# Expert feed-forward on one core: the 64 rest rows of the down product as 64-row products of two row tiles side by side

## The chip, the cores and the metric

The kernel runs on one core of one Trainium2 chip. The metric is the device time of the whole program in microseconds; the median of three runs before the change is 769.99 us (768.62 to 772.36).

## The reference

Cross attention, then a mixture of experts with a residual around each. Only the second half is touched.

```python
x = x + _L0_xattn_ref(_layernorm(x), ctx_2048, mask)          # 16 x 112 tokens of 512
# mixture of experts on the 1792 normed tokens: E = 64, TOP_K = 8, F_INT = 192
probs = softmax(x @ gate_weight.T); top_val, top_idx = lax.top_k(probs, 8)
...                                                           # some experts are rerouted to a similar one
gu = lax.ragged_dot(xs, swapaxes(gate_up_proj, 1, 2), group_sizes)    # 512 -> 2 x 192
gate, up = split(gu, 2)
hact = silu(gate) * up                                        # 192 inner columns for each row
y = lax.ragged_dot(hact, swapaxes(down_proj, 1, 2), group_sizes)      # 192 -> 512
out = zeros.at[tok].add(y * w[:, None])
```

## The kernel before

A first phase (to about 180 us) does the attention, the gate and the choice of experts for 16 batches, and writes a list of tokens and weights for each expert into a table in HBM. A short plan ranks the experts by their number of tokens. The second phase then goes through 63 experts in order of rank; each is a **unit**. `SIZES` gives a unit its number of row tiles `nt` and the rows `m` of a tile: 2 units of 3 x 128, 8 of 3 x 112, 7 of 3 x 96 (17 units of three tiles), then 17 of 2 x 128, 16 of 2 x 112, 12 of 2 x 96 and 1 of 2 x 80 (46 units of two tiles). One more unit of one tile of 128 rows for overflow runs in a loop at the end.

For a unit, SyncE loads the expert's weights into rings of buffers (`load_w1`: three parts of 256 KB into `raw1`, four buffers deep; `load_w2`: 256 KB and 128 KB into `raw2`, three deep). GpSimd gathers the token rows by the list (`gather`) and adds the results back to HBM with an accumulating scatter (`scatter`). Products are made in fp32r with every operand split into a high and a low part, so that each product is a sum of three: high by high, high by low, low by high. ScalarE makes the high parts (`w1_high`, `w2_high`, `h_high`, `x_high`), VectorE the low ones by subtraction (`w1_low`, `w2_low`, `h_low`, `x_low`).

TensorE runs through its program in order: transposes of the token rows (`turn_rows`), 36 products for gate and up (`gate_up`, L1256 to L1258), and, one unit later, the down products (`down`). The order in a round r is: turn rows of unit r+1, `gate_up` of r, `down` of r-1. Each engine has its own program of the same kind, written out by hand, and semaphores connect them. SyncE's program in round r is: list of r+6, w1 of r+4, w2 of r+3; the last waits until VectorE is through `w2_low(r)` (L931).

The inner size is 192 = 128 + 64 (`FR = 64`). The first 128 inner rows of a down tile are three products of 128 rows (L1269 to L1271). The 64 **rest rows** are packed to 128: `hh[:, 1]` holds the high part of h twice (partitions 0 to 63 and 64 to 127, since `h_rest` writes h twice), and `w2h[:, 1]` the high part of the rest weights in partitions 0 to 63 and their low part in 64 to 127. One product of 128 rows (L1273) is thus high by high plus high by low; a second one (L1274) has the low part of h for both. A tile of the down product is five products of 128 rows by 512 columns into one PSUM bank (`y_bank`, a ring of three); ScalarE empties the bank with `y_out` (L1061).

Of the kernel before, what the change touches and what calls it, by code (L numbers as in the profile page):

```python
# [24 lines left out]
F32 = mybir.dt.float32  # L25
F32R = mybir.dt.float32r
# [5 lines left out]
P = 128  # L32
B, T, D = 16, 112, 512
# [7 lines left out]
FR = F - P  # L41
# [28 lines left out]
RAW1, RAW2, LISTS, XGS = 4, 3, 12, 4  # L70
# [76 lines left out]
def program(nc, x, ctx, ctxT, mask, gwT, w1, w2a, w2b, sim, out):  # L147
# [4 lines left out]
    with ExitStack() as stack:  # L152
        def sb(name, shape, dt=F32):
            return stack.enter_context(nc.sbuf_tensor(name, shape, dt))

        def two(name, shape, dt=F32):
            return [sb(f"{name}{i}", shape, dt) for i in range(2)]
# [67 lines left out]
        raw2 = [sb(f"raw2_{i}", [P, 2, D]) for i in range(RAW2)]  # L225
        w1h = [sb("w1h0", [P, DK, 2 * F], F32R)]
        w1l = [sb("w1l0", [P, DK, 2 * F], F32R)]
        w2h = [sb("w2h0", [P, 2, D], F32R)]
        w2l = [sb("w2l0", [P, D], F32R)]
# [33 lines left out]
        early.close()  # L263
        w2h.append(sb("w2h1", [P, 2, D], F32R))
        w2l.append(sb("w2l1", [P, D], F32R))
        w1h.append(sb("w1h1", [P, DK, 2 * F], F32R))
        w1l.append(sb("w1l1", [P, DK, 2 * F], F32R))
        xh = two("xh", [P, DK, WIDE], F32R)
# [3 lines left out]
        hh = two("hh", [P, 2, WIDE], F32R)  # L272
        hl = two("hl", [P, 2, WIDE], F32R)
# [28 lines left out]
        def split_wait(eng, s, value):  # L302

            wait(eng, s, value)
            if not isinstance(value, int):
                eng.sem_inc(spacer, 1)

        def wait(eng, s, value):

            if not isinstance(value, int) or value > 0:  # L310
                eng.wait_ge(s, value)
# [56 lines left out]
        LAST = Unit(STATIC)  # L368
# [5 lines left out]
        def y_bank(u, t):  # L374
            return bank[5 + (u.tile + t) % 3]

        def freed_before(u, t, ring):

            return u.t0 + t if u.loop else max(u.t0 + t - ring + 1, 0)
# [13 lines left out]
        def over_loop(eng, late, early):  # L393

            overs = overs_of(eng)
            with eng.Fori(0, overs) as g:
                late(Unit(STATIC, g))
                early(Unit(STATIC, g + 1))
            return overs
# [5 lines left out]
        def _(sp):  # L405
# [55 lines left out]
            def weights_of(u):  # L461
                at = bass.ds(u.n - STATIC + 2 * E + MAX_OVER, 1) if u.loop else (
                    slice(E + u.n, E + u.n + 1) if u.n < STATIC else slice(2 * E + MAX_OVER, 2 * E + MAX_OVER + 1))
                return sp.value_load(prow[0:1, at], min_val=0, max_val=E - 1)
# [26 lines left out]
            def load_w2(u):  # L491
                split_wait(sp, w2l_s, u.units_freed(RAW2))
                e = weights_of(u)
                sp.dma_start(raw2[u.on(RAW2)][:, 0, :], w2a[bass.ds(e, 1)].rearrange("a p f -> (a p) f")).then_inc(w2_in[u.on(RAW2)], 16)
                sp.dma_start(raw2[u.on(RAW2)][0:FR, 1, :], w2b[bass.ds(e, 1)].rearrange("a p f -> (a p) f")).then_inc(w2_in[u.on(RAW2)], 16)

            load_w1(Unit(0))
            load_w1(Unit(1))
            load_w2(Unit(0))
            load_w1(Unit(2))  # L500
            load_w2(Unit(1))
            load_w1(Unit(3))
            load_w2(Unit(2))
            first_lists = [list_of(Unit(n)) for n in range(3)]
            for i in range(4):
# [18 lines left out]
            overs = over_loop(sp, lambda u: None, next_over)  # L524
# [3 lines left out]
            sp.wait_ge(merged, 16)  # L528
            split_wait(sp, list_in[LAST.on(LISTS)], (overs + LAST.turn(LISTS) + 1) * 16)
            split_wait(sp, w1_in[LAST.on(RAW1)], (overs + LAST.turn(RAW1) + 1) * 16 * W1_PARTS)  # L530
            split_wait(sp, w2_in[LAST.on(RAW2)], (overs + LAST.turn(RAW2) + 1) * 32)
            split_wait(sp, gathered[LAST.on(XGS)][0], (overs + LAST.turn_of_tile(XGS, 0) + 1) * 16)


# [131 lines left out]
        def _(dve):  # L666
            v = nc.vector
# [257 lines left out]
            def w2_low(u):  # L925
                dve.wait_ge(w2h_s, u.n + 1)
                wait(dve, y_ps, u.tiles_freed(2))
                b = u.on(2)
                raw = raw2[u.on(RAW2)]
                v.tensor_tensor(w2l[b][:], raw[:, 0, :], w2h[b][:, 0, :].bitcast(F32), ALU.subtract)  # L930
                v.tensor_tensor(w2h[b][FR:P, 1, :], raw[0:FR, 1, :], w2h[b][0:FR, 1, :].bitcast(F32),  # L931
                                ALU.subtract).then_inc(w2l_s, 1)

            w1_low(Unit(0))
# [2 lines left out]
            for r in range(STATIC):  # L937
                if r < RAMP:
                    stage(h_gate, r)
                    early_stage(x_low, r + 1, (0, 1))  # L940
                    stage(h_rest, r)
                    early_stage(x_low, r + 1, (2,))
                else:
                    early_stage(x_low, r + 1, (0, 1))
                    stage(h_gate, r)
                    early_stage(x_low, r + 1, (2,))
                    stage(h_rest, r)
                stage(w2_low, r)
                early_stage(w1_low, r + 2)
                stage(h_low, r)  # L950

            def late(u):
                h_gate(u)
                h_rest(u)
                w2_low(u)
                h_low(u)
# [9 lines left out]
        def _(act):  # L966
            a = nc.scalar
# [105 lines left out]
                a.copy(w1h[u.on(2)][:].rearrange("p c f -> p (c f)"), raw1[u.on(RAW1)][:]).then_inc(w1h_s, 1)  # L1073

            def w2_high(u):
                act.wait_ge(w2_in[u.on(RAW2)], (u.turn(RAW2) + 1) * 32)
                wait(act, y_ps, u.tiles_freed(2))
                b = u.on(2)
                raw = raw2[u.on(RAW2)]
                a.copy(w2h[b][:, 0, :], raw[:, 0, :])  # L1080
                a.copy(w2h[b][0:FR, 1, :], raw[0:FR, 1, :]).then_inc(w2h_s, 1)

            w1_high(Unit(0))
            w1_high(Unit(1))
# [1 line left out]
            for r in range(STATIC):  # L1086
                if r < RAMP:
                    stage(silu_gate, r)
                    early_stage(x_high, r + 1, (0, 1))
                    stage(w2_high, r)  # L1090
                    stage(silu_rest, r)
                    early_stage(x_high, r + 1, (2,))
                else:
                    early_stage(x_high, r + 1, (0, 1))
                    stage(silu_gate, r)
                    early_stage(x_high, r + 1, (2,))
                    stage(w2_high, r)
                    stage(silu_rest, r)
                early_stage(w1_high, r + 2)
                stage(h_high, r)  # L1100
                stage(y_out, r - 1)
            y_out(Unit(STATIC - 1))

            def late(u):
                silu_gate(u)
                w2_high(u)
                silu_rest(u)
                h_high(u)
                y_out(u)
# [9 lines left out]
        def _(pe):  # L1119
# [141 lines left out]
            def down(u):  # L1261
                b = u.on(2)
                pe.wait_ge(hl_s, u.n + 1)
                pe.wait_ge(w2l_s, u.n + 1)
                for t in range(u.nt):
                    wait(pe, ys_s, freed_before(u, t, 3))
                    s = slice(t * u.m, (t + 1) * u.m)
                    o = y_bank(u, t)[0:u.m, :]
                    pe.matmul(o, hh[b][:, 0, s], w2h[b][:, 0, :], start=True, stop=False)  # L1269
                    pe.matmul(o, hh[b][:, 0, s], w2l[b][:], start=False, stop=False)  # L1270
                    pe.matmul(o, hl[b][:, 0, s], w2h[b][:, 0, :], start=False, stop=False)  # L1271

                    pe.matmul(o, hh[b][:, 1, s], w2h[b][:, 1, :], start=False, stop=False)  # L1273
                    pe.matmul(o, hl[b][:, 1, s], w2h[b][:, 1, :], start=False, stop=True).then_inc(y_ps, 1)  # L1274

            turn_rows(Unit(0), (0, 1, 2))
            for r in range(STATIC):
                if r < RAMP:
                    stage(gate_up, r, 0)
                    stage(gate_up, r, 1)  # L1280
                    early_stage(turn_rows, r + 1, (0, 1))
                    stage(gate_up, r, 2)
                    early_stage(turn_rows, r + 1, (2,))
                else:
                    early_stage(turn_rows, r + 1, (0, 1))
                    stage(gate_up, r, 0)
                    early_stage(turn_rows, r + 1, (2,))
                    stage(gate_up, r, 1)
                    stage(gate_up, r, 2)
                stage(down, r - 1)  # L1290
            down(Unit(STATIC - 1))

            def late(u):
                for m in range(3):
                    gate_up(u, m)
                down(u)
# [42 lines left out]
```

## Time and profile before

| | |
|---|---|
| median of three runs | 769.99 us |
| the profiled execution: its time, its span | 767.57 us, 765.8 us |
| PE, matmul | 661.4 us busy (86%) |
| DVE, ACT, POOL | 542.6 us (71%), 456.7 us (60%), 541.9 us (71%) |
| granted TensorE clock over the span | 0.936 |
| DMA moved | 189.97 MB, mean 248 GB/s |
| raw<-in_w2b (the rest weights) | 65 loads of 128 KB |
| five down products L1269 to L1274 | about 144 of each |

The span is the time from the first to the last instruction of the profiled execution. PE is TensorE's matmuls, PEld its weight loads, SPq the queue of SyncE, which issues the weight loads. A matmul's own length contains the passage through the array, so neighbours overlap; what a product costs in a stream is the distance from its start to the next one's start.

### The profile page before, as it was taken

Reading aid. Unit: us, or ns where it says so; the run is one execution under the profiler, and the core shown is the slowest. Engines: PE = TensorE matmul, PEld = TensorE weight load, DVE = VectorE, ACT = ScalarE, POOL = GpSimd, SP = SyncE. Lnnn points to the kernel's source line nnn. Section 1 sums busy time; section 2 is a strip of 40 time slices with the busy share of each in tenths; the row PEclk is TensorE's granted clock in tenths of the full one; section 3 lists DMA queues with packets and bytes.
Section 4 is the critical chain, followed back from the end, with each engine's and each line's share of the span. In section 5 each row is a group of like instructions: output and inputs, shape, how many; then the busy total and the mean of one; then the engine's idle time right before and its main releaser. Section 6 shows DMA issues by size and latency. Waiting matters only on the chain. (4 is left out here: it accounts for less than half of the span.)

```text
span 765.8 us, 15219 instructions
## 1 busy us (share of the span) xinstructions
PE 661.4 (86%) x4278; PEld 554.9 (72%) x4278; DVE 542.6 (71%) x1213; ACT 456.7 (60%) x891; POOL 541.9 (71%) x463
## 2 busy tenths in 40 slices
PE   4999999831079999999999999999999999999920
PEld 2565555531069988888889999999999999889720
DVE  5598998865047666666677888888887887788611
ACT  3454454312036667667677877778777877768611
POOL 7007777777675877787788888878877888888521
PEclk9999999955579999999999999999999999999975
DMA  8999998615377999999999999999999999999576
GB/s 300 359 326 319 326 349 287 238 44 173 88 208 174 250 230 228 238 227 243 233 246 269 302 289 296 282 273 278 275 274 270 276 274 270 266 273 272 101 143 152
DMA packets 107589, 189.97 MB, mean 248 GB/s; under 512 B 33537, under 2 KB 35457, under 8 KB 106097
## 3 DMA queue, kind: packets, MB, share of 16 engines
q1 hardware_dynamic: 74274, 125.61, 52.0%
q0 software_dynamic: 33232, 63.39, 38.4%
q8 instruction: 35, 0.57, 0.3%
q14 instruction: 48, 0.39, 0.1%
HBM read 143.43 MB, written 56.24 MB: 261 GB/s over the span
## 5 line engine op out<-in xcount | busy, mean ns | idle before, releaser
L1256 PE MATMUL bank<-xh,w1h 128*128 128x256 f32 (+7 forms) x768 | 225.9, 294 | 3.6 <-issue 2.1
L1258 PE MATMUL bank<-xh,w1l 128*128 128x256 f32 (+7 forms) x768 | 220.0, 286 | 0.0
L1257 PE MATMUL bank<-xl,w1h 128*128 128x256 f32 (+7 forms) x768 | 219.9, 286 | 0.0
L617 POOL DMA_INDIRECT xg<-normed_tokens,list x145 | 170.9, 1179 | 59.6 <-issue 55.4
L601 POOL DMA_INDIRECT list_table<-token,slot x112 | 111.6, 996 | 74.4 <-issue 73.7
L626 POOL DMA_INDIRECT out_rows<-ys,list x73 | 123.1, 1686 | 39.7 <-issue 20.1
L1256 PEld LDWEIGHTS bank<-xh,w1h 128*128 128x128 f32 x768 | 147.0, 191 | 4.3 <-issue 4.2
L1257 PEld LDWEIGHTS bank<-xl,w1h 128*128 128x128 f32 x768 | 147.3, 192 | 0.1
L1258 PEld LDWEIGHTS bank<-xh,w1l 128*128 128x128 f32 x768 | 146.9, 191 | 0.0
L626 POOL DMA_INDIRECT second_sum<-ys,list x70 | 117.6, 1680 | 30.3 <-issue 18.6
L922 DVE TENSOR_TENSOR w1l<-raw,w1h 128x1536 fp32r<-128x1536 f32 x65 | 114.3, 1759 | 17.7 <-ACT w1h L1073 16.2
L916 DVE TENSOR_TENSOR xl<-bank,xh 128x448 fp32r<-128x448 f32 (+3 forms) x145 | 84.2, 617 | 50.4 <-ACT xh L1068 48.4
L1235 PE MATMUL bank<-ident,xg 112*128 112x112 f32 (+3 forms) x580 | 71.2, 264 | 52.1 <-DMA xg<-normed_tokens,list 48.5
L1073 ACT CAST w1h<-raw 128x1536 fp32r<-128x1536 f32 x65 | 95.6, 1471 | 30.5 <-DMA raw<-in_w 30.3
L1235 PEld LDWEIGHTS bank<-ident,xg 112*128 112x128 f32 (+3 forms) x580 | 62.7, 143 | 65.7 <-issue 33.7
L1068 ACT CAST xh<-bank 128x448 fp32r<-128x448 f32 (+3 forms) x145 | 69.9, 530 | 57.9 <-PE bank L1235 57.9
L1061 ACT ACTIVATE ys<-bank,list 112x512 f32<-112x512 f32 (+3 forms) x143 | 89.9, 680 | 6.2 <-PE bank L1274 2.1
L899 DVE TENSOR_TENSOR h<-sg,bank 64x256 f32<-64x256 f32 (+6 forms) x64 | 26.6, 416 | 63.2 <-ACT sg L1045 61.8
L1045 ACT ACTIVATE sg<-bank 64x256 f32<-64x256 f32 (+6 forms) x64 | 23.9, 374 | 70.0 <-PE bank L1258 70.0
L1269 PE MATMUL bank<-w2h,hh 128*112 128x512 f32 (+3 forms) x144 | 57.4, 398 | 4.7 <-DVE hl L907 4.7
L1274 PE MATMUL bank<-w2h,hl 128*112 128x512 f32 (+3 forms) x144 | 57.0, 396 | 0.0
L1273 PE MATMUL bank<-w2h,hh 128*112 128x512 f32 (+3 forms) x144 | 56.8, 394 | 0.0
(205 smaller groups left out, 1115.0 us busy)
## 6 DMA issues: line engine op xcount, KB each, us to landing
raw<-in_w SPq DMA_DIRECT2D x195, 256.0 KB, 5.4
raw<-in_w2a SPq DMA_DIRECT2D x65, 256.0 KB
ctxT_s<-in_ctxT SPq DMA_DIRECT2D x16, 768.0 KB, 7.1
ctx_s<-in_ctx SPq DMA_DIRECT2D x16, 768.0 KB, 8.6
raw<-in_w2b SPq DMA_DIRECT2D x65, 128.0 KB
list_table<-blank SPq DMA_DIRECT2D x30, 256.0 KB, 7.4
x_in<-in_x SPq DMA_DIRECT2D x16, 224.0 KB, 5.3
out_rows<-x SPq DMA_DIRECT2D x16, 224.0 KB, 8.3
```

Source lines behind the costliest of these rows:

```text
L601: pool.indirect_dma_start(table, bass.IndirectOffsetOnAxis(ap=slot8[b.four][:, k:k + 1], axis=0), token[b.four][:, k, :], None).then_inc(t ...
L617: pool.indirect_dma_start(xg[u.on(XGS)][0:u.m, t, :], None, normed, bass.IndirectOffsetOnAxis(ap=lists[u.on(LISTS)][0:u.m, t, 0:1], axis=0 ...
L626: pool.indirect_dma_start((out, second)[u.sums()], bass.IndirectOffsetOnAxis(ap=lists[u.on(LISTS)][0:u.m, t, 0:1], axis=0), ys[u.on(2)][0: ...
L916: v.tensor_tensor(xl[u.on(2)][:, :, part], turned(u, t), xh[u.on(2)][:, :, part].bitcast(F32), ALU.subtract).then_inc(xl_s, 1)
L922: v.tensor_tensor(w1l[u.on(2)][:].rearrange("p c f -> p (c f)"), raw1[u.on(RAW1)][:], w1h[u.on(2)][:].rearrange("p c f -> p (c f)").bitcas ...
L1061: a.activation(ys[u.on(2)][0:u.m, t, :], y_bank(u, t)[0:u.m, :], ACT.Copy, scale=of_row).then_inc(ys_s, 1)
L1068: a.copy(xh[u.on(2)][:, :, t * u.m:(t + 1) * u.m], turned(u, t)).then_inc(xh_s, 1)
L1073: a.copy(w1h[u.on(2)][:].rearrange("p c f -> p (c f)"), raw1[u.on(RAW1)][:]).then_inc(w1h_s, 1)
L1235: mm = pe.transpose(turned(u, t)[:, c, :], xg[u.on(XGS)][0:u.m, t, c * P:(c + 1) * P], ident[0:u.m, 0:u.m])
L1256: pe.matmul(bank[m][:, 0:W], wh, mh, start=(c == 0), stop=False)
L1257: pe.matmul(bank[m][:, 0:W], wh, ml, start=False, stop=False)
L1258: mm = pe.matmul(bank[m][:, 0:W], wl, mh, start=False, stop=(c == DK - 1))
```

## The change

The rest weights are loaded twice, into partitions 0 to 63 and 64 to 127 of `raw2[:, 1]`. ScalarE rounds all 128 partitions, and VectorE writes the low part of the rest weights into a buffer of its own, `w2r`, again for both halves. In `down` the rest rows are now three products of 64 rows for a tile: a tile with an even number takes partitions 0 to 63, one with an odd number 64 to 127. For tiles 0 and 1 of a unit the products alternate between the halves; tile 2, where there is one, follows alone. The 64-row products come first in a bank's sum, the three of 128 rows after them, and both banks of a pair are waited for ahead of the first.

```diff
+        w2r = two("w2r", [P, D], F32R)
...
-                sp.dma_start(raw2[u.on(RAW2)][0:FR, 1, :], w2b[bass.ds(e, 1)].rearrange("a p f -> (a p) f")).then_inc(w2_in[u.on(RAW2)], 16)
+                for half in (slice(0, FR), slice(FR, P)):
+                    sp.dma_start(raw2[u.on(RAW2)][half, 1, :], w2b[bass.ds(e, 1)].rearrange("a p f -> (a p) f")).then_inc(w2_in[u.on(RAW2)], 16)
...
-                v.tensor_tensor(w2h[b][FR:P, 1, :], raw[0:FR, 1, :], w2h[b][0:FR, 1, :].bitcast(F32),
+                v.tensor_tensor(w2r[b][:], raw[:, 1, :], w2h[b][:, 1, :].bitcast(F32),
                                 ALU.subtract).then_inc(w2l_s, 1)
...
-                a.copy(w2h[b][0:FR, 1, :], raw[0:FR, 1, :]).then_inc(w2h_s, 1)
+                a.copy(w2h[b][:, 1, :], raw[:, 1, :]).then_inc(w2h_s, 1)
...
-                for t in range(u.nt):
-                    wait(pe, ys_s, freed_before(u, t, 3))
-                    s = slice(t * u.m, (t + 1) * u.m)
-                    o = y_bank(u, t)[0:u.m, :]
-                    pe.matmul(o, hh[b][:, 0, s], w2h[b][:, 0, :], start=True, stop=False)
-                    pe.matmul(o, hh[b][:, 0, s], w2l[b][:], start=False, stop=False)
-                    pe.matmul(o, hl[b][:, 0, s], w2h[b][:, 0, :], start=False, stop=False)
-
-                    pe.matmul(o, hh[b][:, 1, s], w2h[b][:, 1, :], start=False, stop=False)
-                    pe.matmul(o, hl[b][:, 1, s], w2h[b][:, 1, :], start=False, stop=True).then_inc(y_ps, 1)
+                for ts in ((0, 1), (2,)):
+                    ts = [t for t in ts if t < u.nt]
+                    for t in ts:
+                        wait(pe, ys_s, freed_before(u, t, 3))
+                    for i, (rows, weights) in enumerate(((hh[b], w2h[b][:, 1, :]), (hh[b], w2r[b][:]), (hl[b], w2h[b][:, 1, :]))):
+                        for t in ts:
+                            half = slice(t % 2 * FR, (t % 2 + 1) * FR)
+                            pe.matmul(y_bank(u, t)[0:u.m, :], rows[half, 1, t * u.m:(t + 1) * u.m], weights[half, :],
+                                      start=(i == 0), stop=False)
+                    for t in ts:
+                        s = slice(t * u.m, (t + 1) * u.m)
+                        o = y_bank(u, t)[0:u.m, :]
+                        pe.matmul(o, hh[b][:, 0, s], w2h[b][:, 0, :], start=False, stop=False)
+                        pe.matmul(o, hh[b][:, 0, s], w2l[b][:], start=False, stop=False)
+                        pe.matmul(o, hl[b][:, 0, s], w2h[b][:, 0, :], start=False, stop=True).then_inc(y_ps, 1)
```

On TensorE, a unit of two tiles of 128 rows has these down products before; a row names what is written and read and the size of the result (in the diff's new lines all 64-row products have one line, L1274, and `x2` stands for two in a row).

```order
L1269 MATMUL bank<-w2h,hh 128x512
L1270 MATMUL bank<-w2l,hh 128x512
L1271 MATMUL bank<-w2h,hl 128x512
L1273 MATMUL bank<-w2h,hh 128x512
L1274 MATMUL bank<-w2h,hl 128x512
L1269 MATMUL bank<-w2h,hh 128x512
L1270 MATMUL bank<-w2l,hh 128x512
L1271 MATMUL bank<-w2h,hl 128x512
L1273 MATMUL bank<-w2h,hh 128x512
L1274 MATMUL bank<-w2h,hl 128x512
```

The same place of the change, between the last gate_up product of the next unit and the transposes of the one after:

```order
L1260 MATMUL bank<-xh,w1l 128x256
L1274 MATMUL bank<-w2h,hh 128x512 x2
L1274 MATMUL bank<-w2r,hh 128x512 x2
L1274 MATMUL bank<-w2h,hl 128x512 x2
L1279 MATMUL bank<-w2h,hh 128x512
L1280 MATMUL bank<-w2l,hh 128x512
L1281 MATMUL bank<-w2h,hl 128x512
L1279 MATMUL bank<-w2h,hh 128x512
L1280 MATMUL bank<-w2l,hh 128x512
L1281 MATMUL bank<-w2h,hl 128x512
L1237 MATMUL bank<-ident,xg 128x112 x8
```

Ten products of 128 rows have become six of 64 rows, in three pairs, and six of 128 rows: TensorE goes once from 128 rows to 64 and once back.

On TensorE, the third tile of a unit of three tiles of 112 rows ends the unit's down products in the change like this:

```order
L1274 MATMUL bank<-w2h,hh 112x512
L1274 MATMUL bank<-w2r,hh 112x512
L1274 MATMUL bank<-w2h,hl 112x512
L1279 MATMUL bank<-w2h,hh 112x512
L1280 MATMUL bank<-w2l,hh 112x512
L1281 MATMUL bank<-w2h,hl 112x512
```

It has six products where it had five, and TensorE goes to 64 rows and back a second time in such a unit.

On SyncE's queue, the loads of w2 of one unit and the list of the next in the change (`raw_2` is a buffer of the ring; before, the second line of the loads has no `x2`):

```order
L495 DMA raw_2<-in_w2a 128x512
L497 ISA
L497 DMA raw_2<-in_w2b 64x512 x2
L468 TENSOR_LOAD prow
L468 ISA x2
L482 ISA
L482 DMA list<-list_table 96x3x16
```

One load of 64 rows of 2 KB has been put between w2 and the next unit's list and w1, on the same queue.

## Rows read from the trace of the kernel before

**Rows 1.** Stretches of the second phase: length, busy time by engine, clock, DMA share, GB/s.

```profile
core 0: us, PE busy (x) PEld busy (x) DVE busy (x) ACT busy (x) POOL busy (x), PEclk, DMA share, GB/s
300.00:400.00 100.00, 97.40 (x637) 85.17 (x636) 69.46 (x101) 70.22 (x123) 76.85 (x58) 1.00 0.97 237
400.00:500.00 100.00, 100.00 (x731) 93.72 (x730) 82.70 (x121) 77.59 (x136) 83.56 (x54) 1.00 1.06 287
500.00:600.00 100.00, 100.00 (x756) 92.07 (x755) 82.22 (x125) 76.98 (x139) 79.88 (x55) 1.00 1.05 273
600.00:700.00 100.00, 99.20 (x763) 89.68 (x762) 81.03 (x129) 76.24 (x143) 81.85 (x57) 1.00 1.03 272
```

**Rows 2.** Timeline of PE, down of one two-tile unit: start, length, line, tiles, rows*columns.

```profile
508.77 0.40 PE L1269 MATMUL bank<-w2h,hh 128*128 128x512 f32 x1
...
509.91 0.39 PE L1269 MATMUL bank<-w2h,hh 128*128 128x512 f32 x1
...
511.05 0.36 PE L1235 MATMUL bank<-ident,xg 112*128 112x112 f32 x2
```

**Rows 3.** Timeline of PE, first phase: into and out of a 2-row product.

```profile
99.69 0.66 PE L1162 MATMUL bank<-gw_s,xn2T 128*112 128x64 f32 x5
...
100.18 0.26 PE L1162 MATMUL bank<-gw_s,xn2T 128*112 128x64 f32 x1
100.38 0.23 PE L1171 MATMUL bank<-list_base,ones_b 2*112 2x64 bf16 x1
100.54 0.24 PE L1172 MATMUL bank<-mk,tri 112*112 112x64 bf16 x1
100.61 0.22 PE L1173 MATMUL bank<-run,minus 112*112 112x64 bf16 x1
```

**Rows 4.** Timeline of PE, first phase: into and out of a 16-row product.

```profile
98.28 0.55 PE L1133 MATMUL bank<-ident,xn 112*128 112x112 f32 x4
...
101.34 0.26 PE L1126 MATMUL bank<-ident,probs 112*128 112x112 f32 x1
101.53 0.36 PE L1143 MATMUL bank<-masked,of_batch 16*112 16x375 bf16 x1
101.82 0.88 PE L1145 MATMUL bank<-ctxT_s,xnT 128*112 128x375 f32 x2
...
103.80 0.79 PE L1145 MATMUL bank<-ctxT_s,xnT 128*112 128x375 f32 x2
```

**Rows 5.** DMA from 400 to 500 us: queue, packets, MB, share; one issue's KB, us to landing.

```profile
q1 hardware_dynamic: 11995, 15.60, 48.4%
list<-list_table SPq DMA_DIRECT2D x10, 16.0 KB, 4.9
```

**Rows 6.** The same from 600 to 700 us.

```profile
q1 hardware_dynamic: 12116, 17.15, 57.7%
list<-list_table SPq DMA_DIRECT2D x11, 12.0 KB, 13.8
```

**Rows 7.** Waits from 500 to 600 us: us in total, times, longest.

```profile
ACT w1h L1073 <- DMA raw<-in_w: 7.3, 5, 2.1
```

**Rows 8.** Waits from 600 to 700 us.

```profile
ACT w1h L1073 <- DMA raw<-in_w: 15.2, 10, 3.5
```

**Rows 9.** Timeline around 655 us: ACT's longest wait and PE after it.

```profile
655.17 1.48 ACT L1073 CAST w1h<-raw 128x1536 fp32r<-128x1536 f32 x1 [3.53 <-DMA raw<-in_w]
...
658.96 0.47 PE L1269 MATMUL bank<-w2h,hh 128*96 128x512 f32 x1 [0.80 <-DVE hl L907]
```

**Rows 10.** Timeline around 503 us: VectorE's low parts of w2, and the load.

```profile
502.89 0.69 DVE L930 TENSOR_TENSOR w2l<-raw,w2h 128x512 fp32r<-128x512 f32 x1
503.60 0.71 DVE L931 TENSOR_TENSOR w2h<-raw,w2h 64x512 fp32r<-64x512 f32 x1
...
505.60 0.57 SPq L495 DMA_DIRECT2D raw<-in_w2b  x1
```

**Rows 11.** SyncE's queue from 500 to 700 us: its waits.

```profile
SPq L464 <- DVE w2h L931: 40.9, 26, 2.9
```

More of the change, by code:

```diff
@@ L530, in _ @@
             split_wait(sp, w1_in[LAST.on(RAW1)], (overs + LAST.turn(RAW1) + 1) * 16 * W1_PARTS)
-            split_wait(sp, w2_in[LAST.on(RAW2)], (overs + LAST.turn(RAW2) + 1) * 32)
+            split_wait(sp, w2_in[LAST.on(RAW2)], (overs + LAST.turn(RAW2) + 1) * 48)
             split_wait(sp, gathered[LAST.on(XGS)][0], (overs + LAST.turn_of_tile(XGS, 0) + 1) * 16)
@@ L1075, in w2_high @@
             def w2_high(u):
-                act.wait_ge(w2_in[u.on(RAW2)], (u.turn(RAW2) + 1) * 32)
+                act.wait_ge(w2_in[u.on(RAW2)], (u.turn(RAW2) + 1) * 48)
                 wait(act, y_ps, u.tiles_freed(2))
```

## The prediction

> **What bounds the kernel now.** I read the slices and stretches first, since an average over the span mixes the attention phase with the expert phase. From 400 to 600 us TensorE is busy for the whole of each 100 us, from 300 to 400 us for 97.4 of them, at a granted clock of 1.00, the upper of its two levels (2.4 GHz) [rows 1]. VectorE (82), ScalarE (77) and GpSimd (80) have some 18 to 23 us in 100 to spare. So in the expert phase TensorE's stream sets the pace, and a product that goes out of it shortens a round.
>
> Next the timeline of one unit's down products, for the price of one. Ten products start at 508.77 and the next work at 511.05 [rows 2]: 0.228 us each, and nothing stands between them. Their own length of 0.39 us is not the price; it contains the passage through the array.
>
> Then DMA, because the share in the same stretches is about 1 [rows 1]. Read alone this number says little, since it adds packets that are under way together. The time from issue to landing says more. A list of 16 KB, which queues behind the weights of the unit before on SyncE's queue, lands 4.9 us after its issue between 400 and 500 us [rows 5]; a smaller one takes 13.8 us between 600 and 700 us [rows 6]. That is a queue that is never empty: a round there is about 7.1 us. The chain of waits shows who feels it. ScalarE waits for the weights w1 five times between 500 and 600 us, 2.1 us at most, and TensorE does not notice [rows 7, 1]. Between 600 and 700 us it waits ten times [rows 8], once for 3.53 us, and this time the low part of h is late and TensorE waits 0.80 us for it [rows 9]. So from about 565 us on the transfers are level with TensorE, and the slack that hides a late w1 is between 2.1 and 3.5 us.
>
> **The change, part by part.** *Products.* A pair of tiles has ten full steps of 0.228 now [rows 2]. If the two halves run side by side, it has three steps for the six 64-row products and six for the others, so nine: 0.23 us less. The third tile of a three-tile unit has six steps for five, 0.23 more; such a unit is even at 15 steps. If the halves don't run side by side, a pair has twelve steps. No row of the trace has two products in different halves of the array, so these are the bounds, three steps and six. I take three, because the halves use separate partitions and separate banks, and keep six as a rival. One sentence of the Trainium skill bears on it (TensorE: Matmul & The Clock Gate, the table of measured speedups in its part on packing): four row tiles of 32 rows ran 3.07 times faster than in sequence, so they took 1.30 of one. By that a pair of steps would take somewhat over one; at an estimated 1.1, 63 pairs with three such steps each would add 4.3 us. No run here shows it yet.
>
> *Going to 64 rows and back.* The first phase has the nearest rows: products of few rows between full ones. L1162 repeats every 0.10 us ((0.66 - 0.26) / 4), but from the last one to the 2-row L1171 it is 0.20; from L1171 to L1172 it is 0.16, to L1173 after it 0.07 [rows 3]. That is 0.10 in and 0.09 out. With the 16-row L1143: transposes repeat every 0.097 us ((0.55 - 0.26) / 3), the last takes 0.19; L1143 to L1145 is 0.29 where 375 columns are at most 375/512 of 0.228 = 0.17; and the first two L1145 take 0.88 where later ones take 0.79 [rows 4]. That is 0.09 in and 0.12 + 0.09 out. A round trip thus costs 0.19 to 0.30 us; I take the middle, 0.245, since it is unknown which of the two a 64-row product resembles. A two-tile unit makes one trip: -0.228 + 0.245 = about +0.02 us. A three-tile unit makes two: +0.49 us, and 17 of them +8.3 us.
>
> The Trainium skill has a rule for this (TensorEngine Tiling (Array Packing), Key Properties): a change of the tiling mode drains the array. If a drain is what a lone product takes beyond its place in the stream, 0.39 - 0.23 = 0.16 us, twice in a trip makes 0.32 and the whole sum below about 22 us instead of 17.7. The rows are a little cheaper than that rule, and they decide.
>
> *The second load of the rest weights.* 128 KB (0.131 MB) more for each unit on SyncE's queue. Between 600 and 700 us 17.15 MB take 57.7% of 16 engines for 100 us [rows 6]: 0.131 / 17.15 x 57.7 = 0.44 us of all engines. Between 400 and 500 us 15.60 MB take 48.4% [rows 5]: 0.41 us. By the bytes at 272 GB/s [rows 1] it is 0.48. Where the transfers are level with TensorE this lengthens each round, once the slack of 2 to 3.5 us is used up; that is some 22 units, those from 565 us to the end of the phase at about 722. I take 0.41: 9.0 us. Nothing, the lower bound, would hold if the long landings came from the order in the queue and not from full engines; against it stands that the backlog, once there, stays for 18 units, and that a wait of 3.5 us did reach TensorE. Before 565 us a longer queue costs nothing: w1 is issued over 14 us ahead of its use.
>
> *Parts at nothing.* VectorE's subtraction on 64 partitions takes 0.71 us, on 128 partitions 0.69 [rows 10], so `w2r` costs what it replaces, and ScalarE's rounding likewise. The issue of the load takes SyncE 0.57 us [rows 10]; its queue waits 40.9 us in 26 waits for `w2_low` [rows 11], 1.6 us each, which covers it. Behind it on that queue stand the next list and w1, which are issued that much later. Tile 0 of a pair is finished after nine of twelve products, not five of ten; ScalarE comes to `y_out` only after `w1_high` and `h_high`, when both tiles are done. The wait for both banks ahead of the pair finds them emptied a round before.
>
> **The sum.** 17 x 0.49 = 8.3; 24 two-tile units ahead of the backlog x 0.017 = 0.4; 22 x 0.41 = 9.0: +17.7 us. Made on the profiled execution (767.57 us, span 765.8 and 1.8 around it) this is 785.3; that execution was 2.4 us under the median of 769.99, so the median after is 787.7, say 788.
>
> **Rivals.** (a) *The load is hidden.* Then only the trips count: 8.3 + 46 x 0.017 = 9.1 us, 779. For it: TensorE was still fully busy between 500 and 600 us with waits on w1 under way. Against: the 3.53 us wait. (b) *The halves don't run side by side*: a two-tile unit +0.456 + 0.245 = 0.70, a three-tile one +0.684 + 0.49 = 1.17; 46 x 0.70 + 17 x 1.17 = 52 us, 822. TensorE would then be slow enough to hide the load. This is the case that the change doesn't do what it says. For it: no row shows two products at once. (c) *Faster*: the weight load of the first product after a switch is hidden and the trip is cheap. At no cost 46 x 0.228 = 10.5 us go, 759. There are 46 + 34 = 80 trips, so it breaks even at 10.5 / 80 = 0.13 us a trip, if the load is hidden too; under 0.083 it is a gain of more than 0.5%. The place is down; for it speaks only that a product of 2 rows is short and may show the switch worse than a long one, against it that the long 16-row one cost more.
>
> **Chances.** Forecast 0.46: between 0.19 a trip with 0.3 a load (6.5 - 0.9 + 6.6 = 12 us, 782) and 0.30 with 0.48 for 28 units (10.2 + 1.3 + 13.4 = 25, 795), and up to 802 if a side-by-side step loses 15% (63 x 3 x 0.034 = 6.5). (a) 0.22: 775 to 786. (b) 0.12: 815 to 830. (c) 0.13: 759 to 766. In between, a trip of 0.08 to 0.18 with the load hidden, 0.07: 766 to 774. What differs by over 0.5% (3.9 us) can be told from no change here. Faster 0.13, same 0.08 (the last case and the edges), slower 0.79. The range of 762 to 802 leaves out (b) and half of (c). The forecast's own range is 782 to 802.
>
> **What would show it.** In the timeline of a two-tile unit the two products of a pair start within some 0.1 us of each other and the next pair 0.23 us later; if starts are 0.23 apart throughout, (b) holds. The first 64-row product and the first 128-row one after them stand 0.09 to 0.2 us further from their forerunners than others. In the stretches, units of three tiles take 0.4 to 0.6 us longer each, those of two tiles before 500 us the same as now. After 565 us ScalarE's waits for w1 grow and TensorE's waits for the low part of h become regular, with rounds of about 7.5 us; the list's landing goes over 14 us earlier than now. Wrong would be: rounds of 7.1 us after 565 us (no cost of the load), or of 6.9 (cheap switches).

## The result, and the profile after

The changed kernel takes 793.9 us (median, 792.4 to 795.9), the kernel before 769.55 (768.6 to 772.4): a ratio of 1.0327, with 1.0294 to 1.0359 as its interval, or some 24 us more. The profiled execution took 793.95 us with a span of 792.2.

The stretches of the second phase after (columns as in [rows 1]):

```profile
300.00:400.00 100.00, 100.00 (x647) 80.55 (x647) 65.03 (x98) 68.38 (x118) 74.00 (x56) 1.00 0.99 244
400.00:500.00 100.00, 100.00 (x728) 87.77 (x727) 78.50 (x116) 74.85 (x130) 78.53 (x53) 1.00 1.07 289
500.00:600.00 100.00, 96.33 (x734) 84.29 (x734) 74.14 (x115) 68.98 (x124) 73.22 (x52) 1.00 1.05 270
600.00:700.00 100.00, 94.61 (x736) 81.53 (x735) 73.61 (x117) 69.81 (x131) 77.21 (x53) 1.00 1.03 271
```

Two things differ from [rows 1]. Up to 500 us TensorE is fully busy, and in the first stretch it now is where it had 2.6 us of idle time; so what was lost there was lost inside its stream. From 500 us on it is idle for 3.7 and 5.4 us, where it had 0 and 0.8. The granted clock is 1.00 throughout, so none of it is the clock's.

The stream itself, in the timeline of TensorE (start, length, line, tiles, rows*columns). First a unit of two tiles of 128 rows, from the last gate_up product on:

```profile
440.94 0.28 PE L1260 MATMUL bank<-xh,w1l 128*128 128x256 f32 x1
441.15 0.50 PE L1274 MATMUL bank<-w2h,hh 64*128 64x512 f32 x2
441.49 0.40 PE L1274 MATMUL bank<-w2r,hh 64*128 64x512 f32 x2
441.71 0.40 PE L1274 MATMUL bank<-w2h,hl 64*128 64x512 f32 x2
442.04 0.50 PE L1279 MATMUL bank<-w2h,hh 128*128 128x512 f32 x1
442.37 0.39 PE L1280 MATMUL bank<-w2l,hh 128*128 128x512 f32 x1
442.61 0.40 PE L1281 MATMUL bank<-w2h,hl 128*128 128x512 f32 x1
```

Each `x2` row has two products that start together: the row is 0.40 us long, as one product alone is. The halves do run side by side. Now read the distances of the starts. A step without a switch is 0.22 to 0.24 (the third pair from the second, the last row from the one before). Four are longer: the gate_up products stand 0.12 apart, and the first pair comes 0.21 after the last of them (+0.09); the second pair comes after 0.34 (+0.11), the first full product after 0.33 (+0.10), the second full one after 0.33 (+0.10). A switch is paid twice, at the first product and again at the next, and a trip has two switches. Over whole units these four are 0.37 us, worked out with the rounds below; [rows 3] had shown 0.19 for a trip.

The weight loads (PEld) of the same unit show what the two parts are:

```profile
441.14 0.19 PEld L1274 LDWEIGHTS bank<-w2h,hh 64*128 64x128 f32 x2
441.25 0.19 PEld L1274 LDWEIGHTS bank<-w2r,hh 64*128 64x128 f32 x2
...
442.38 0.19 PEld L1281 LDWEIGHTS bank<-w2h,hl 128*128 128x128 f32 x1
```

Inside the stream a load goes in ahead: that of L1281 starts at 442.38, its product at 442.61. At the switch it starts only with its product, at 441.14, 0.09 after the place of a product without a switch: that is the first part. From it to the next load, at 441.25, 0.11 passes, which no earlier product hides: that is the second. At the switch back it is the same, at 442.04.

A unit of three tiles makes the trip twice:

```profile
311.35 0.32 PE L1260 MATMUL bank<-xh,w1l 128*128 128x336 f32 x1
311.59 0.48 PE L1274 MATMUL bank<-w2h,hh 64*112 64x512 f32 x2
311.92 0.40 PE L1274 MATMUL bank<-w2r,hh 64*112 64x512 f32 x2
...
313.73 0.40 PE L1281 MATMUL bank<-w2h,hl 128*112 128x512 f32 x1
314.05 0.48 PE L1274 MATMUL bank<-w2h,hh 64*112 64x512 f32 x1
314.38 0.39 PE L1274 MATMUL bank<-w2r,hh 64*112 64x512 f32 x1
...
314.93 0.49 PE L1279 MATMUL bank<-w2h,hh 128*112 128x512 f32 x1
315.26 0.39 PE L1280 MATMUL bank<-w2l,hh 128*112 128x512 f32 x1
```

The third tile's three steps (314.05 to 314.93) are for one tile alone, and the same 0.32 to 0.34 stand at its entry and its exit.

Then the idle time. The chain of waits between 500 and 600 us (who waits, for whom: us in total, times, longest):

```profile
ACT w1h L1075 <- DMA raw<-in_w: 22.3, 9, 3.7
...
PE bank L1274 <- DVE hl L909: 3.7, 4, 1.7
```

and between 600 and 700 us:

```profile
ACT w1h L1075 <- DMA raw<-in_w: 32.6, 14, 3.9
...
PE bank L1274 <- DVE hl L909: 5.4, 8, 1.3
```

ScalarE waits for w1 twice as long as in [rows 8], and TensorE's waits for the low part of h are, to the tenth, the time that it lacks in the stretches: 3.7 and 5.4 us. One more of 2.0 us comes at 703 us, 11.1 in all. The transfers from 600 to 700 us (as [rows 6]):

```profile
q1 hardware_dynamic: 12494, 17.41, 58.4%
...
list<-list_table SPq DMA_DIRECT2D x12, 12.0 KB, 12.8
```

It moves hardly more than before in the same time (17.41 MB for 17.15, at 271 GB/s for 272), though each unit asks for 0.131 MB more, and the rounds become longer. The list's landing here is no longer than the 13.8 us of [rows 6]; it grew earlier. Between 520 and 560 us it is, before and after:

```profile
list<-list_table SPq DMA_DIRECT2D x6, 14.0 KB, 11.9
list<-list_table SPq DMA_DIRECT2D x5, 14.0 KB, 16.4
```

To see which unit pays, I took the start of the first gate_up product of every unit from the trace; a round is the distance of two such starts. Means in us, in the order of the program, for the profiled executions of the kernel before, after, and of the experiments below:

```
                        3 tiles   3 tiles   2 tiles   2 tiles   2 tiles
rows of a tile              112        96       128       112        96
units                       2-9     10-16     17-33     34-49     50-61
before                    10.57      9.72      7.52      7.10      7.06
after                     10.98      9.96      7.73      7.77      7.53
first load only           10.98      9.96      7.73      7.25      7.10
before + second load      10.57      9.73      7.52      7.83      7.12
all in one half           11.68     10.66      8.41      7.93      7.79
before, rest on 64 rows   10.67      9.77      7.89      7.47      7.33
```

The excess over before is 3.3 + 1.7 us in the three-tile stages (8 x 0.41, 7 x 0.24), 3.6 in the first two-tile one (17 x 0.21), and 10.7 + 5.6 in the last two (16 x 0.67, 12 x 0.47): 25 us of the 26 by which the two spans differ. In the last two stages the load does not lengthen every round: 13 of the 28 are 0.2 to 3.6 us longer than the same round with the first load only, and the other 15 are within 0.02 us of it. The first late one starts at 543 us.

### The profile page after: what moved, and what is told of

Its sections match the earlier page's. It is cut to its first block and busy times, and to the rows that moved or that the text cites. A ratio compares the mean times of both kernels' runs of the same rounds, so it can differ in the third digit from the quotient of the medians.

```text
span 792.2 us, 15699 instructions
## 1 busy us (share of the span) xinstructions
PE 682.7 (86%) x4422; PEld 544.3 (69%) x4422; DVE 535.6 (68%) x1213; ACT 456.4 (58%) x891; POOL 537.5 (68%) x463
## 5 line engine op out<-in xcount | busy, mean ns | idle before, releaser
L619 POOL DMA_INDIRECT xg<-normed_tokens,list x145 | 169.0, 1165 | 59.9 <-issue 56.0
L628 POOL DMA_INDIRECT out_rows<-ys,list x73 | 120.5, 1651 | 54.2 <-ACT ys L1063 37.9
L1279 PE MATMUL bank<-w2h,hh 128*112 128x512 f32 (+3 forms) x144 | 64.9, 451 | 0.0
L895 DVE TENSOR_TENSOR h<-sg,bank 128x256 f32<-128x256 f32 (+6 forms) x64 | 26.3, 410 | 49.9 <-issue 32.3
L1281 PE MATMUL bank<-w2h,hl 128*112 128x512 f32 (+3 forms) x144 | 57.7, 400 | 0.0
```

The source lines that it names most:

```text
L619: pool.indirect_dma_start(xg[u.on(XGS)][0:u.m, t, :], None, normed, bass.IndirectOffsetOnAxis(ap=lists[u.on(LISTS)][0:u.m, t, 0:1], axis=0 ...
L628: pool.indirect_dma_start((out, second)[u.sums()], bass.IndirectOffsetOnAxis(ap=lists[u.on(LISTS)][0:u.m, t, 0:1], axis=0), ys[u.on(2)][0: ...
```

## The experiments

Each is compared with runs of the kernel before on the same chip, whose medians were 768.3 to 769.5 us; the ratios are to them.

**Which part costs what.** The first keeps the products of the change and drops the second load after the first units, so the upper half of the partitions then holds the rest weights of an early unit, and the results are those of other weights:

```
-                for half in (slice(0, FR), slice(FR, P)):
+                for half in ((slice(0, FR), slice(FR, P)) if not u.loop and u.n < RAW2 else (slice(0, FR),)):
```

> The change without its second load of the rest weights after the first three units (the second half of the buffers then holds old weights, so every odd tile's rest rows use wrong weights; the work of the engines is the same). Theory (the load costs about 12 us once the transfers are level with TensorE): rounds of two-tile units after 510 us go back to about 7.27 and 7.14 us, ScalarE's waits for w1 fall to what they were before the change, and the whole is 780 to 784 us. Rival (the loss after 500 us is TensorE's own): 792 to 796 us.

It took 782.6 us, 1.0169 (1.0143 to 1.0196). The stretches:

```profile
500.00:600.00 100.00, 100.00 (x767) 88.10 (x765) 79.97 (x122) 75.65 (x136) 75.90 (x53) 1.00 1.05 268
600.00:700.00 100.00, 100.00 (x782) 86.60 (x781) 78.84 (x126) 76.64 (x140) 81.08 (x56) 1.00 1.02 272
```

TensorE has no idle time left, so the waits of the change were those of the load, and what the load adds to the products is 793.9 - 782.6 = 11.3 us. The products alone add 13.1, and the table has them in every stage: 0.41, 0.24, 0.21, 0.15 and 0.04 us a round (0.12 in the last without unit 53, whose 8.07 us before hold the wait of [rows 9]).

The reverse: the products of before, with the load twice (into rows that nothing reads):

```
-                sp.dma_start(raw2[u.on(RAW2)][0:FR, 1, :], w2b[bass.ds(e, 1)]...)
+                for half in (slice(0, FR), slice(FR, P)):
+                    sp.dma_start(raw2[u.on(RAW2)][half, 1, :], w2b[bass.ds(e, 1)]...)
```

> The kernel before with the second load of the rest weights alone; nothing reads it. Theory (a round cannot be shorter than the transfers allow, 7.5 to 7.8 us in the last 28 two-tile units): 782 to 789 us, with TensorE waiting for the low part of h after 500 us. By the price in the prediction (22 units at 0.41 us) 779 us. Rival (the load is hidden when TensorE's products are as before): 768 to 772 us.

787.0 us, 1.0231 (1.0206 to 1.0257): the load alone adds 17.5, far more than the 9 of the prediction. Its chain of waits between 600 and 700 us shows the change's pattern with before's products:

```profile
ACT w1h L1074 <- DMA raw<-in_w: 24.4, 13, 3.6
...
PE bank L1270 <- DVE hl L908: 3.9, 4, 1.7
```

The two parts give 13.1 + 17.5 = 30.6 us apart and 24.4 together. That slower products leave the load more time shows further down: with all products in one half, and rounds of 7.93 and 7.79 us, ScalarE does not wait for w1 at all between 500 and 700 us. Where the 6 us between sum and whole go is not shown; the table can't divide them, since the profiled execution of the second load alone was the fastest of its five (782.4 us).

Is it the 0.131 MB, or one more transfer and its issue on the queue? Before, with a second load of 16 columns (4 KB in place of 128) into rows that nothing reads:

```
+                sp.dma_start(raw2[u.on(RAW2)][FR:P, 1, 0:16], w2b[bass.ds(e, 1), :, 0:16]...)
```

> The kernel before with a second load of the rest weights cut to 16 of 512 columns (4 KB for each unit in 64 pieces); nothing reads it. Theory (the second load costs by its bytes): 768 to 773 us, TensorE fully busy from 400 to 600 us. Rival (it costs as one more transfer in the queue ahead of the list and w1): 780 us or more.

Its ratio is 1.0034 (1.0005 to 1.0062), some 3 us and 5 at most, of 17.5: most of the cost goes with the bytes.

**Side by side or not.** The change, with all 64-row products in the lower half:

```
-                            half = slice(t % 2 * FR, (t % 2 + 1) * FR)
+                            half = slice(0, FR)
```

> The change with both tiles of a pair in partitions 0 to 63 (the sums are the same). Theory (two 64-row products run side by side because they are in different halves of the array): a pair takes six steps, each two-tile round is 0.69 us longer, 8.3 us for 2 x 128, TensorE sets every round and hides the load: 822 to 830 us. Rival (the start times in the trace do not show what the products cost, and the halves don't matter): 792 to 796 us.

824.3 us, 1.0711 (1.0682 to 1.0740). In the timeline a pair takes two steps:

```profile
440.92 0.62 PE L1274 MATMUL bank<-w2r,hh 64*128 64x512 f32 x2
441.39 0.62 PE L1274 MATMUL bank<-w2h,hl 64*128 64x512 f32 x2
441.94 0.50 PE L1279 MATMUL bank<-w2h,hh 128*128 128x512 f32 x1
```

The rows start 0.47 us apart instead of 0.22. So the second half is worth 30 us to the change, and 41.6 to its products alone (824.3 - 782.6), where 63 pairs with three steps each make 63 x 3 x 0.228 = 43: what it promised it does, and it lost by other terms.

Then the order. The change writes a pair as the same product of tile 0 and tile 1 in turn; here all three of tile 0 come first, then the three of tile 1:

```
-                    for i, (rows, weights) in enumerate(...):
-                        for t in ts:
+                    for t in ts:
+                        for i, (rows, weights) in enumerate(...):
```

> The change with the 64-row products of a pair in another order: the three of tile 0, then the three of tile 1, each tile still in its own half. Theory (products start in program order, and only neighbours in different halves run side by side): the third of tile 0 and the first of tile 1 overlap, so five steps where the change has three, 0.46 us more for each round, 11.4 us for 3 x 112, 8.1 for 2 x 128, and the load is hidden by the longer rounds: 808 to 814 us. Rival (the order of a pair's products does not matter, a half takes its next product as soon as it is free): 792 to 796 us.

My theory, that products of the same half then stand one behind the other, fell: 797.1 us, 1.0361 (1.0316 to 1.0407), 3 us from the change and not 15. The timeline:

```profile
441.68 0.51 PE L1274 MATMUL bank<-w2h,hh 64*128 64x512 f32 x2
442.02 0.40 PE L1274 MATMUL bank<-w2r,hh 64*128 64x512 f32 x2
442.25 0.40 PE L1274 MATMUL bank<-w2h,hl 64*128 64x512 f32 x2
442.58 0.50 PE L1279 MATMUL bank<-w2h,hh 128*128 128x512 f32 x1
```

The program has hh, w2r, hl of tile 0 and then hh, w2r, hl of tile 1; the trace has two of each starting together. So the other half's products started up to three places ahead of their turn. The order here is that of kernel.py; the trace doesn't number the instructions, and that nothing between the two changed the order was not tested. In the experiment with the trip alone, below, 64-row products that share a half stand in the order of kernel.py.

**The price of a trip.** The kernel before, whose two rest products of each tile (128 rows, high and low weights stacked) use the lower 64 rows alone and come first; the product with the low rest weights is thereby left out, and the count of products stays at five a tile:

```
-                    pe.matmul(o, hh[b][:, 1, s], w2h[b][:, 1, :], start=False, stop=False)
-                    pe.matmul(o, hl[b][:, 1, s], w2h[b][:, 1, :], start=False, stop=True).then_inc(y_ps, 1)
...
+                for t in range(u.nt):
+                    pe.matmul(o, hh[b][0:FR, 1, s], w2h[b][0:FR, 1, :], start=True, stop=False)
+                    pe.matmul(o, hl[b][0:FR, 1, s], w2h[b][0:FR, 1, :], start=False, stop=False)
+                for t in range(u.nt):
...
```

> The kernel before with its two rest products of each tile put ahead of the unit's others and cut to the first 64 rows (the low part of the rest weights is left out): as many steps as before, one load, one trip to 64 rows and back for each unit. Theory (a trip costs about 0.37 us: the first product on either side starts 0.09 late and its weights are loaded in the open for another 0.09): two-tile rounds of 7.83 (2 x 128), 7.48 and 7.37 us, three-tile rounds 0.1 to 0.37 longer, 787 to 793 us. By the price in the prediction (0.245): 782. Rival (no cost of the trip; the loss comes from more products): 768 to 772 us.

786.1 us, 1.0215 (1.0187 to 1.0244). Five steps a tile and no second load, so in the table the difference to before is one trip, or a cover for it: 0.37 us in units of two tiles of 128 and of 112 rows, and 0.36 at 96 (without unit 53; the means of the table, which hold it, differ by 0.27). In the timeline:

```profile
445.17 0.28 PE L1258 MATMUL bank<-xh,w1l 128*128 128x256 f32 x1
445.38 0.50 PE L1270 MATMUL bank<-w2h,hh 64*128 64x512 f32 x1
445.72 0.39 PE L1271 MATMUL bank<-w2h,hl 64*128 64x512 f32 x1
445.95 0.40 PE L1270 MATMUL bank<-w2h,hh 64*128 64x512 f32 x1
...
446.50 0.50 PE L1275 MATMUL bank<-w2h,hh 128*128 128x512 f32 x1
446.84 0.39 PE L1276 MATMUL bank<-w2l,hh 128*128 128x512 f32 x1
447.07 0.39 PE L1277 MATMUL bank<-w2h,hl 128*128 128x512 f32 x1
```

0.34 from the first 64-row product to the second, 0.23 to the third; 0.34 from the first full one to the second, 0.23 to the third: the four exposures again, without a pair in sight. I had expected the three-tile rounds to grow by 0.1 to 0.37; they grew by 0.10 and 0.05. Since this kernel also changes the order, its twin keeps the order and goes back to 128 rows, with nothing left out:

```
-                    pe.matmul(o, hh[b][0:FR, 1, s], w2h[b][0:FR, 1, :], start=True, stop=False)
+                    pe.matmul(o, hh[b][0:P, 1, s], w2h[b][0:P, 1, :], start=True, stop=False)
```

> The kernel before with its two rest products of each tile put ahead of the unit's others, all of 128 rows as before: the order of the run with the trip alone, without the trip. Theory: 768 to 772 us, so the whole difference of that run is the trip. Rival (the order itself costs, through later finished tiles or the wait for all banks): over 775 us.

1.0003 (0.9983 to 1.0023): the order is free, and the 16 us are the 64 rows.

What hides a trip in a three-tile unit stands in the timeline of before:

```profile
314.58 0.32 PE L1258 MATMUL bank<-xh,w1l 128*128 128x336 f32 x1
315.16 0.53 PE L1235 MATMUL bank<-ident,xg 96*128 96x96 f32 x4 [0.26 <-DVE xl L916]
```

and at such a place after, one unit earlier:

```profile
307.27 0.31 PE L1260 MATMUL bank<-xh,w1l 128*128 128x336 f32 x1
307.42 0.55 PE L1237 MATMUL bank<-ident,xg 112*128 112x112 f32 x4
```

Ahead of the transposes of the third tile TensorE waited for VectorE's `x_low`: 0.58 us from start to start, where now it is 0.15. In the units from 4 to 15 it is 0.56 to 0.82 before and 0.13 to 0.15 after. A longer down gives VectorE that time, so of 0.74 us for two trips some 0.4 to 0.5 was idle time before, and 0.2 to 0.4 is left. This is the 2.6 us that the stretch from 300 to 400 us got back. Four rounds show the trips without this cover: those of units 2 and 3, where the wait is not there before (0.16 us from start to start), and of 16 and 17, which have the down of a three-tile unit but no third tile to transpose. They grew by 0.82, 0.72, 0.68 and 0.68 us, two trips.

**One trip in place of two.** All three tiles go to 64 rows together, once without the second load (same other weights as above) and once with it:

```
-                for ts in ((0, 1), (2,)):
+                for ts in ((0, 1, 2),):
```

> The change without the second load (as in the first run of this study: odd tiles use old rest weights) and with all 64-row products of a three-tile unit ahead of its full ones, so one trip for every unit. Theory (a trip costs 0.37 us, and a wait ahead of the third tile's transposes hides part of it in three-tile units): three-tile rounds as with the trip alone, 10.7 and 9.8 us, two-tile rounds as without the second load; 777 to 780 us. Rival (three-tile rounds are set by another engine, so a trip more or less does not show): 781 to 784 us.

> The change with all 64-row products of a three-tile unit ahead of its full ones: one trip for every unit, both loads. Theory (17 trips fewer at 0.37 us, all of it in three-tile rounds, which the transfers don't set): 787 to 789 us, three-tile rounds of 10.6 and 9.7 us. Rival (the earlier end of the three-tile stage is lost again in the stage that the transfers set): 792 to 795 us.

Without the load the ratio is 1.0088 (1.0059 to 1.0117), with it 1.0251 (1.0207 to 1.0295, 789.2 us). Against 1.0169 the first is 0.81%, or 6.2 us, better: 0.37 for each of 17 units, one trip. Its three-tile rounds are 10.62 and 9.63 us, about those of before. With the load 4.7 of these 6.2 us remain (793.9 - 789.2), from four runs that spread from 785.5 to 792.6.

**The copy on the chip.** One load only; ScalarE rounds the rest weights into both halves and VectorE subtracts twice, with one trip. It computes everything:

```
-                a.copy(w2h[b][:, 1, :], raw[:, 1, :]).then_inc(w2h_s, 1)
+                a.copy(w2h[b][0:FR, 1, :], raw[0:FR, 1, :])
+                a.copy(w2h[b][FR:P, 1, :], raw[0:FR, 1, :]).then_inc(w2h_s, 1)
...
-                v.tensor_tensor(w2r[b][:], raw[:, 1, :], w2h[b][:, 1, :].bitcast(F32),
+                v.tensor_tensor(w2r[b][0:FR], raw[0:FR, 1, :], w2h[b][0:FR, 1, :].bitcast(F32), ALU.subtract)
+                v.tensor_tensor(w2r[b][FR:P], raw[0:FR, 1, :], w2h[b][0:FR, 1, :].bitcast(F32),
```

> The change with one load of the rest weights, whose second half ScalarE and VectorE make on the chip (one more rounding and one more subtraction of 64 partitions for each unit), and with one trip for every unit; it computes all of the reference. Theory (TensorE sets the rounds at 10.6, 7.7, 7.25 and 7.1 us, and some 20 us in 100 that the two engines have to spare cover 0.6 to 0.7 us more in each round): 774 to 779 us. Rival (VectorE, at 80 us in 100, or the longer way from h to its low part becomes the bound in two-tile rounds): 785 us or more.

The theory fell: 785.6 us, 1.0213 (1.0190 to 1.0237). That run left no profile of a usual execution, so the kernel ran again for one.

> The same kernel as the copy on the chip once more, for its profile. The measured 785.6 us against the expected 774 to 779 leave some 10 us. If VectorE or ScalarE sets the rounds, two-tile rounds are longer than without the load from 2 x 128 on, TensorE waits for the low part of h or the low part of w1, and one of the two is busy for over 90 us in 100. If it is the transfers again, the 2 x 128 rounds are 7.7 us, ScalarE waits for w1, and the loss is after 500 us.

787.7 us, 1.0226 (1.0121 to 1.0331). The two-tile rounds are nearly those of the experiment with one trip and no load (7.71, 7.36, 7.10 against 7.70, 7.26, 7.10). The loss is in the three-tile ones: 11.17 and 10.28 us instead of 10.62 and 9.63. The stretch from 300 to 400 us, and its waits:

```profile
300.00:400.00 100.00, 95.08 (x628) 79.84 (x627) 68.60 (x103) 72.69 (x123) 76.62 (x54) 1.00 0.93 219
```

```profile
PEld bank L1239 <- issue: 6.9, 9, 1.0
ACT xh L1071 <- PE bank L1239: 6.4, 9, 0.9
PE bank L1239 <- DVE xl L918: 4.9, 9, 0.8
```

It is the wait ahead of the third tile's transposes once more, 4.9 us in nine rounds, and it is VectorE's: the added subtraction stands ahead of `x_low` in its stream. In the round that starts at 286.9 us VectorE has no idle time from it to the second `x_low`, and the first `x_low` starts 1.78 us into the round, where it is 0.97 with one trip and no load (unit 6 in both); `x_high` starts 0.09 into it in both. ScalarE and VectorE are busy for some 70 of 100 us, and still one more operation of 0.7 us at that place is late. I had costed it at nothing by those shares.

No version was faster than before. In a two-tile unit none with one pair for each trip can be by these numbers: the pair saves one step, 0.228 us, and the trip costs 0.36 to 0.37. Only in units of three tiles of 96 rows, where the wait ahead of the transposes hides the one trip, did a round become shorter, 9.63 us for 9.72.

## Why the prediction was right, and where its terms were off

The sign, the bounds and the range held: slower, by a trip per unit and by a load, with the halves side by side. The median came 6 us above the 788 forecast. By its steps:

- *Three steps for the six products of a pair*: right. Products of a pair start within 0.01 us of each other and pairs follow at 0.22 to 0.24. By the Trainium skill's table (TensorE: Matmul & The Clock Gate, Measured speedup vs the span model; four row tiles) I had estimated 1.1 steps and 4.3 us more; with two tiles of 64 rows the trace shows 1.0, and the trace decides.
- *A trip at 0.245 us*: this is the term that was mis-sized. It measured 0.37 in units of two tiles of 112 and 128 rows, above the range of 0.19 to 0.30 from [rows 3, 4], since each switch is paid at two products, not one. The larger of those rows did show a second exposure on the way out, 0.12 + 0.09; I took the middle instead. The rule of the Trainium skill that a change of tiling mode drains the array (TensorEngine Tiling (Array Packing), Key Properties) was read as 0.32 a trip; that was nearer, though still low, and the four exposures, not two, are what the trace shows.
- *Two-tile rounds before the backlog as they were (+0.017)*: wrong by that term. A trip of 0.37 less a step of 0.228 is +0.14; the rounds without the second load show 0.15 at 112 rows, 0.12 at 96 (without unit 53) and 0.21 at 128, where unit 17 with its 0.68 is in the mean. In the table that is 6.4 us for 45 units, where I had 0.8 for 46.
- *Three-tile units +0.49, 8.3 us*: it came out lower (0.41 and 0.24, about 5 us), by two errors against each other: trips of 0.74, and a wait ahead of the third tile's transposes that covered 0.4 to 0.5 of them and that I had not looked for. The 2.6 us of idle time in [rows 1] was its trace.
- *The load at 9.0 us*: it added 11.3 to the slower products, and 17.5 alone. Its cause was right, down to the wait of TensorE for the low part of h. The step that was wrong is that it lengthens each round by its 0.41 us: 13 of 28 rounds were late, by 0.2 to 3.6 us each, and the others not at all. That the sum came near is luck in part. The backlog also began ahead of 565 us: ScalarE's first wait for w1 of over 1 us is at 535 us (568 before), and the first late round starts at 543. The list's landing went over 14 us earlier than before, as I had said: 16.8 us for the list issued at 524 us, where before the first such is issued at 635. After 560 us it was back under 14 us, and what grew were the waits for w1.
- *The parts at nothing*: they hold. The issue of the load is bounded by the small second load, some 3 us and 5 at most, and the order by its twin's 1.0003.
- *The rivals*: a hidden load (a) is excluded by the two load experiments; products not side by side (b) would have given the 824 us of the experiment in one half, near the 822 worked out, where the low price of a trip and the wait that was overlooked cancel; a gain (c) needed trips under 0.13 us.

So the total held because errors had different signs. Of the 25 us in the table the three-tile rounds are 5.0 (forecast 8.3), the products in two-tile rounds 6.4 (forecast 0.4), and the load 13.5 (forecast 9.0).

What stays open: why single transfers come late. With the load alone the rounds over 7.5 us are scattered, some of 9 or 10.7 us among others of 7.1, and the profile does not say which packet was behind. Nor is it shown why the weights of the first product after a switch do not go in ahead; only that they don't.

## What to carry to other kernels

Count the switches between 64 and 128 rows before the products: here a trip costs one and a half full products, so pairs in two halves should pay only if two or more pairs share a trip (worked out; no run here has that), or if a wait hides it. Where TensorE and the transfers are level, take the price of a second copy of data by its bytes at the rate of that stretch for a low one: it came to 9.0 us here, and 11.3 and 17.5 were measured. The costs of two changes need not add there either: these were 30.6 us apart and 24.4 together. Idle time of a nearly full engine, even 2.6% as here, can belong to one place; find it first, since added work was free there and a late helper was dear.

## What the runs showed of the hardware

- Two fp32r products of 64 rows and 512 columns in different halves start within 0.01 us of each other and take together what one takes: 30 us between the change and the same with one half.
- Such products start out of the order of kernel.py: written tile by tile, they still start in pairs of two tiles (441.68, 442.02, 442.25 above), up to three places ahead of their turn, and the time moves by 3 us and not by the 15 or more that I had worked out for waiting. The Trainium skill says the opposite (TensorE: Matmul & The Clock Gate, Step-by-step: what each phase is for): only weight loads are pulled ahead, matmuls stay in program order. For products of two halves the trace shows otherwise, as far as the order of kernel.py is the one that reached the chip, and the trace decides.
- A trip from 128 rows to 64 and back costs 0.37 us at a granted clock of 1.00, in four parts of 0.09 to 0.11: the first product after each switch and the one after it. The weights of that first product go in with it (441.14 and 441.15), where in a stream they go in 0.23 us ahead (442.38 and 442.61).
